# Four and a half chunks of twelve transposed by DMA instead of four

## The reference

```
layer 0:  s = x W0 inp^T, where adj > 0, else a very negative number
          x1 = layernorm(x + softmax(s / 0.07) inp)
layer 1:  Wh = x1 W;  e_ij = leaky_relu(Wh_i a1 + Wh_j a2), where adj > 0, else very negative
          out = layernorm(x1 + elu(softmax(e) Wh))
```

## Time and profile before

| | us |
|---|---|
| median of 3 executions | 1432.35 (1432.2 to 1432.74) |
| profiled execution | 1431.7 |
| its span, first to last instruction | 1429.9 |

### The profile page before, as it was taken

The page is one execution under the profiler, slowest core; times in us unless marked ns, Lnnn a source line. Parts: engine busy times, 40 slices in busy tenths (PEclk is TensorE's granted clock), DMA queues, the critical chain, the costliest instruction groups (busy, mean ns, idle before and its releaser), DMA issues.

```text
span 1429.9 us, 28561 instructions
## 1 busy us (share of the span) xinstructions
PE 1404.5 (98%) x9695; PEld 1012.5 (71%) x9695; DVE 1288.6 (90%) x2170; ACT 1103.4 (77%) x2477; POOL 1192.8 (83%) x895
## 2 busy tenths in 40 slices
PE   8999999999999999999999999999999999999997
PEld 4677777777777777777777777776666666676764
DVE  6999999999999999999899999979999999999997
ACT  6788888888888888888888888887856665666564
POOL 6878888888888888888888878857989999999995
PEclk9999999999999999999999999999999999999999
DMA  8999999999999999999899999857444444443520
GB/s 269 295 276 270 257 265 252 272 273 274 263 255 262 267 267 276 267 264 264 254 272 269 274 261 257 249 99 143 92 94 91 104 102 103 98 109 85 108 59 16
DMA packets 431761, 294.06 MB, mean 206 GB/s; under 512 B 360064, under 2 KB 406400, under 8 KB 431616
## 3 DMA queue, kind: packets, MB, share of 16 engines
q1 hardware_dynamic: 431616, 292.24, 75.5%
HBM read 163.19 MB, written 40.92 MB: 143 GB/s over the span
## 4 chain that ended last, share of the span: by engine, by line
PE 93%; DVE 3%; issue 1%; ACT 1%; POOL 1%; DMA 0%; POOLq 0%; DVEq 0%; SPq 0%; ACTq 0%
PE ps L698 17%; PE ps L783 12%; PE ps L727 12%; PE ps L793 11%; PE ps L700 9%; PE ps L738 8%; PE ps L740 8%; PE ps L739 8%; PE ps L764 6%; DVE rows L1130 1%; PE ps L665 1%; PE ps L807 1%; POOL p_lo L601 1%; DVE neg_mask L1095 1%; PE ps L658 0%
## 5 line engine op out<-in xcount | busy, mean ns | idle before, releaser
L935 ACT ACTIVATE rows<-rows,exp_bias 128x512 f32<-128x512 f32 x576 | 417.1, 724 | 55.9 <-DVE exp_bias L1105 55.8
L601 POOL TENSOR_TENSOR p_lo<-p,p_hi 128x1024 fp32r<-128x1024 f32 x171 | 403.0, 2406 | 26.6 <-ACT p_hi L983 22.9
L1130 DVE CUSTOM_DVE_ANT_0 rows<-ps,neg_mask 128x1024 f32<-128x1024 f32 x288 | 352.1, 1223 | 79.6 <-PE ps L740 72.1
L509 POOL TENSOR_SCALAR edges<-neg_mask 128x1536 uint8<-128x1536 bf16 x190 | 307.3, 1617 | 95.8 <-DVE neg_mask L1095 83.9
L1226 DVE SCALAR_TENSOR_TENSOR p<-ps,e_col,edgesT 128x1024 f32<-128x1024 f32 x288 | 348.8, 1274 | 5.6 <-ACT ps L988 4.6
L698 PE MATMUL ps<-vals,pT_hi 128*128 128x256 f16 x1536 | 294.6, 273 | 0.2
L921 ACT CAST pT_hi<-ps 128x512 f16<-128x512 f32 x384 | 222.9, 580 | 89.7 <-PE ps L727 89.5
L551 POOL TENSOR_TENSOR inp_sb<-rows,inp_sb 128x512 f16<-128x512 f32 x192 | 281.6, 1486 | 8.2 <-DVE inp_sb L1139 0.7
L700 PE MATMUL ps<-vals,pT_lo 128*128 128x128 f16 x1536 | 274.1, 219 | 0.0
L983 ACT CAST p_hi<-p 128x1024 fp32r<-128x1024 f32 x191 | 195.0, 1047 | 97.6 <-DVE p L1226 92.3
L1146 DVE TENSOR_TENSOR pT_lo<-ps,pT_hi 128x512 f16<-128x512 f32 x384 | 250.7, 683 | 3.7 <-ACT pT_hi L921 3.7
(11 more groups left out here) (130 smaller groups left out, 1934.7 us busy)
## 6 DMA issues: line engine op xcount, KB each, us to landing
adj_sb<-adj SPq DMA_DIRECT2D x192, 768.0 KB, 5.6
edge_rows<-edges SPq DMA_DIRECT2D x192, 192.0 KB, 4.8
xq<-x SPq DMA_DIRECT2D x48, 64.0 KB, 2.9
xr<-x SPq DMA_DIRECT2D x48, 64.0 KB, 5.7
r_wide<-r_rows SPq DMA_DIRECT2D x5, 512.0 KB, 4.0
out<-y_w SPq DMA_DIRECT2D x5, 512.0 KB, 3.7
inp_sb<-inp SPq DMA_DIRECT2D x3, 768.0 KB, 8.0
inp_sb<-inp_sb SPq DMA_TRANSPOSE x96, 4.6
```

What stands on the lines that cost most here:

```text
L601: nc.gpsimd.tensor_tensor(p1_lo[:, m % LO_SLOTS, :], p1[:, (NB * g + n) % P_SLOTS, :], p1_hi[:, m % HI_SLOTS, :].bitcast(F32), ALU.subtrac ...
L935: nc.scalar.activation(row_chunk(1 - par, c), row_chunk(1 - par, c), ACT.Exp, bias=exp_bias[:, 1 - par:2 - par], scale=EXP_SCALE, accum_ou ...
L1130: nc.vector.tensor_tensor_reduce(row_pair(par, k), scores_pair(k), neg_mask_row[:, 2 * k * CHUNK:2 * (k + 1) * CHUNK], 1.0, -3.0e38, ALU.a ...
```

## The change

The DMA way now takes four chunks and the first two of the four blocks of chunk 4 (EXTRA = 2): 2304 columns instead of 2048, in five pieces (PIECES), the fifth 256 wide. TensorE turns only the other two blocks of chunk 4, and the cast and the subtraction of this turn are 256 wide. ScalarE's fifth cast is at step 7; GpSimd's fifth low part stands between the fourth and the edges of the next tile. The product of the two blocks moves from chunk 4's attend (step 9) to that of chunk 3 (step 8). The waits that counted four pieces count five. `moved_lo` has a buffer of its own; `s_prod` lies in the end of the space of `inp_sb`.

```diff
+EXTRA = 2
-        MW = MOVED * CHUNK
+        PIECES = MOVED + 1
+        MW = MOVED * CHUNK + EXTRA * P
-        moved_hi, moved_lo = (inp_space[:, i * MW:(i + 1) * MW] for i in range(2))
-        movedT = inp_space[:, 2 * MW:6 * MW].rearrange(...)
+        moved_hi = inp_space[:, 0:MW]
+        moved_lo = sb0("moved_lo", [P, MW], F16)[:]
+        movedT = inp_space[:, MW:5 * MW].rearrange(...)
-        s_prod = sb0("s_prod", [P, 2, P], F32)
+        s_prod = inp_sb[:, NB - 2:NB, :]
+        def moved_piece(of, i):
+            return of[:, i * CHUNK:min((i + 1) * CHUNK, MW)]
+        def moved_rows(par, i):
+            return rows[:, par * N + i * CHUNK:par * N + min((i + 1) * CHUNK, MW)]
+        def turned_part(bc):
+            return slice(EXTRA * P if bc == MOVED else 0, CHUNK)
 # SP
-                    sp.wait_ge(moved_hi_set, MOVED * (tile + 1))
+                    sp.wait_ge(moved_hi_set, PIECES * (tile + 1))
-                    sp.wait_ge(moved_lo_set, MOVED * (tile + 1))
+                    sp.wait_ge(moved_lo_set, PIECES * (tile + 1))
 # GpSimd
-                if tile == 0:
-                    pool.wait_ge(vals_lo, MOVED)
-                nc.gpsimd.tensor_tensor(moved_lo[:, i * CHUNK:(i + 1) * CHUNK], row_chunk(tile % 2, i),
-                                        moved_hi[:, i * CHUNK:(i + 1) * CHUNK], ALU.subtract)
+                nc.gpsimd.tensor_tensor(moved_piece(moved_lo, i), moved_rows(tile % 2, i), moved_piece(moved_hi, i),
+                                        ALU.subtract)
                     moved_low(t - 1, 2)
                     moved_low(t - 1, 3)
+                    moved_low(t - 1, 4)
 # TensorE: attend, then the turn
-                for b in range(BPC):
-                    jb = bc * BPC + b
+                first = bc * BPC + (EXTRA if bc == MOVED else 0)
+                last = (bc + 1) * BPC + (EXTRA if bc == MOVED - 1 else 0)
+                for jb in range(first, last):
-                        for b in range(BPC):
+                        for b in range(EXTRA if bc == MOVED else 0, BPC):
 # ScalarE
-                        nc.scalar.copy(pT_hi[:, n % PT_SLOTS, :], ps[:, PT0 + n % NPT, :])
-                    if 0 <= c - LAG < MOVED and 1 <= t < NB:
+                        part = turned_part(bc)
+                        nc.scalar.copy(pT_hi[:, n % PT_SLOTS, part], ps[:, PT0 + n % NPT, part])
+                    if 0 <= c - LAG < PIECES and 1 <= t < NB:
 # VectorE
-                            if 2 * k < MOVED:
-                                dve.wait_ge(moved_lo_set, MOVED * (t - 1))
+                            if 2 * k <= MOVED:
+                                dve.wait_ge(moved_lo_set, PIECES * (t - 1))
-                        nc.vector.tensor_tensor(pT_lo[:, s, :], ps[:, PT0 + n % NPT, :], pT_hi[:, s, :],
+                        part = turned_part(bc)
+                        nc.vector.tensor_tensor(pT_lo[:, s, part], ps[:, PT0 + n % NPT, part], pT_hi[:, s, part],
```

More of the change, by code:

```diff
@@ L98, in build @@
         pT_lo = sb0("pT_lo", [P, PT_SLOTS, CHUNK], F16)
-        MW = MOVED * CHUNK
+        PIECES = MOVED + 1
+        MW = MOVED * CHUNK + EXTRA * P
         inp_space = inp_sb[:].bitcast(F16).rearrange("p b d -> p (b d)")
-        moved_hi, moved_lo = (inp_space[:, i * MW:(i + 1) * MW] for i in range(2))
-        movedT = inp_space[:, 2 * MW:6 * MW].rearrange("p (s h b m) -> p s h b m", s=2, h=2, m=P)
+        moved_hi = inp_space[:, 0:MW]
+        moved_lo = sb0("moved_lo", [P, MW], F16)[:]
+        movedT = inp_space[:, MW:5 * MW].rearrange("p (s h b m) -> p s h b m", s=2, h=2, m=P)
         xq = sb0("xq", [P, P], F32)
@@ L536, in score_cols @@
                 after(pool, s_set, j)
-                nc.gpsimd.tensor_tensor(s_prod[:], x1.rearrange("p (a d) -> p a d", a=1).to_broadcast([P, 2, P]), wa_rep[:],
+                nc.gpsimd.tensor_tensor(s_prod, x1.rearrange("p (a d) -> p a d", a=1).to_broadcast([P, 2, P]), wa_rep[:],
                                         ALU.mult).then_inc(s_prod_set, 1)
@@ L545, in moved_low @@
             def moved_low(tile, i):
-                pool.wait_ge(moved_hi_set, MOVED * tile + i + 1)
-                if tile == 0:
-                    pool.wait_ge(vals_lo, MOVED)
+                pool.wait_ge(moved_hi_set, PIECES * tile + i + 1)
                 if tile >= 1:
                     pool.wait_ge(movedT_in[(tile - 1) % 2], movedT_loads(tile - 1))
-                nc.gpsimd.tensor_tensor(moved_lo[:, i * CHUNK:(i + 1) * CHUNK], row_chunk(tile % 2, i),
-                                        moved_hi[:, i * CHUNK:(i + 1) * CHUNK], ALU.subtract).then_inc(moved_lo_set, 1)
+                nc.gpsimd.tensor_tensor(moved_piece(moved_lo, i), moved_rows(tile % 2, i), moved_piece(moved_hi, i),
+                                        ALU.subtract).then_inc(moved_lo_set, 1)
             def tile_rstd(t, par, known):
@@ L679, in attend @@
                 if t_of == 0:
-                    pe.wait_ge(vals_lo, bc + 1)
+                    pe.wait_ge(vals_lo, bc + 2 if bc == MOVED - 1 else bc + 1)
                     pe.wait_ge(wa_copied, 1)
@@ L692, in attend @@
                 acc = tile_sum(t_of)
-                for b in range(BPC):
-                    jb = bc * BPC + b
-                    cols = slice(b * P, (b + 1) * P)
+                first = bc * BPC + (EXTRA if bc == MOVED else 0)
+                last = (bc + 1) * BPC + (EXTRA if bc == MOVED - 1 else 0)
+                for jb in range(first, last):
+                    cols = slice((jb - bc * BPC) * P, (jb - bc * BPC + 1) * P)
                     p_hi = movedT[:, t_of % 2, 0, jb, :] if by_dma else pT_hi[:, s, cols]
                     p_lo = movedT[:, t_of % 2, 1, jb, :] if by_dma else pT_lo[:, s, cols]
-                    nc.tensor.matmul(acc, p_hi, vals[:, jb, :], start=(bc == MOVED and b == 0), stop=False,
+                    nc.tensor.matmul(acc, p_hi, vals[:, jb, :], start=(jb == MOVED * BPC + EXTRA), stop=False,
                                      skip_group_check=True)
                     mm = nc.tensor.matmul(acc[:, P:2 * P], p_lo, vals[:, jb, 0:P], start=False,
-                                          stop=(bc == MOVED - 1 and b == BPC - 1), skip_group_check=True)
+                                          stop=(jb == MOVED * BPC + EXTRA - 1), skip_group_check=True)
                 mm.then_inc(pv_done, 1)
@@ L920, in tile_steps @@
                             act.wait_ge(pv_done, attend_number((n - PT_SLOTS) // TURNS, (n - PT_SLOTS) % TURNS + MOVED) + 1)
-                        nc.scalar.copy(pT_hi[:, n % PT_SLOTS, :], ps[:, PT0 + n % NPT, :]).then_inc(pT_hi_set, 1)
-                    if 0 <= c - LAG < MOVED and 1 <= t < NB:
+                        part = turned_part(bc)
+                        nc.scalar.copy(pT_hi[:, n % PT_SLOTS, part], ps[:, PT0 + n % NPT, part]).then_inc(pT_hi_set, 1)
+                    if 0 <= c - LAG < PIECES and 1 <= t < NB:
                         i = c - LAG
@@ L928, in tile_steps @@
                             act.wait_ge(movedT_in[t % 2], movedT_loads(t - 2))
-                        nc.scalar.copy(moved_hi[:, i * CHUNK:(i + 1) * CHUNK], row_chunk(1 - par, i)).then_inc(moved_hi_set, 1)
+                        nc.scalar.copy(moved_piece(moved_hi, i), moved_rows(1 - par, i)).then_inc(moved_hi_set, 1)
                     if known is None or 1 <= known <= NB:
@@ L1134, in tile_steps @@
                         row_bias(t, par, known)
-                    if t == NB and 0 <= c - LAG < MOVED:
+                    if t == NB and 0 <= c - LAG < PIECES:
                         i = c - LAG
@@ L1138, in tile_steps @@
                         dve.wait_ge(movedT_in[t % 2], movedT_loads(t - 2))
-                        nc.vector.tensor_copy(moved_hi[:, i * CHUNK:(i + 1) * CHUNK], row_chunk(1 - par, i)).then_inc(moved_hi_set, 1)
+                        nc.vector.tensor_copy(moved_piece(moved_hi, i), moved_rows(1 - par, i)).then_inc(moved_hi_set, 1)
                     if turn_at(known, c):
```

## The result

The change makes the kernel slower: 1447.17 us (median of 4, 1446.42 to 1447.57) against 1432.28 us (median of 4), ratio 1.0104 (95% interval 1.0086 to 1.0121). The profiled execution took 1447.0 us, its span is 1445.2 us, 15.3 more than before. TensorE's granted clock is 0.996, as before.

The account below looks back on a forecast made before the run. A GpSimd-VectorE loop, 19.11 + 0.72 = 19.83 us per tile, was to overtake TensorE: 45 x 0.475 = 21.4, less 1.5 at the end, on 1431.7 gives 1451.6, 1452.3 as median. Range 1436 to 1462, likeliest case 1443 to 1461.

Parts of the forecast that it names:

- The ring becomes the bound: Per tile: the GpSimd-VectorE loop grows from 19.11 to 19.83 us, above TensorE's 19.14; +0.47 over 19.36; chance 0.70.
- The term of GpSimd's fifth part: GpSimd's new 256-wide low part, ahead of edges and sum: 0.65 us plus 0.07 of waiting, 0.72 per tile.
- the mask's wait: GpSimd's low parts beside VectorE's mask: the mask still delays the fourth, costing about 0.07 us more per tile.
- The end, -1.5 us: End of the first layer: TensorE's lead of up to 1 us and 0.22 in each of two last tiles save 1.5.
- the ring: Once-per-tile loop: GpSimd from mask to sum, VectorE from bn_stats to next mask; 19.11 us before the change.
- TensorE alone at 19.14: TensorE per tile: two of 32 transposes fewer save 0.22 us, so its own work falls from 19.36 to 19.14.
- rival A: Steps 8 to 11: the mask waits past the fourth low part, TensorE stays the bound, 1422 us; chance 0.13.
- ScalarE, VectorE, DMA at no cost: Casts under 0.1 us more, pT_lo 0.3 less, DMA work 19.1 per tile, later landing with 2.8 us left: hidden.
- rival C: Step 3: longer DMA transposes land 2.8 us later and ScalarE waits; above 1462 us; chance 0.05.

Follow-up runs that it names:

- before_extra_low: The kernel before, plus one 256-column GpSimd subtraction into an unread buffer, which the second DMA transpose and the masks' additions await: 1447.56 us, 1.0105.
- after_sum_first: The changed kernel with GpSimd's two additions of x and the product moved ahead of the next tile's two edges: 1435.46 us, 1.0024 to before.
- after_low_by_vector: The changed kernel with the fifth low part taken from GpSimd and given to VectorE at the end of step 9: 1434.38 us, 1.0015 to before.
- the dose: The kernel before with an extra GpSimd subtraction 32, 128 or 256 columns wide: 1431.89, 1435.87 and 1447.56 us.
- after_sum_lo_first: The changed kernel with GpSimd's two additions ahead of the edges and VectorE's step-9 pT_lo ahead of the mask's addition: 1420.68 us, 0.9919 to before.

## Why the prediction was right, and where it was off

*The ring becomes the bound.* Right, and shown three ways: before_extra_low makes the loss alone, after_sum_first and after_low_by_vector take most of it away, and the dose has a threshold near 0.26 with a slope of one beyond it. Its length of 19.11 without the new part stands: 19.68 - 0.56 = 19.12.

*The term of GpSimd's fifth part.* Mis-sized: 0.56 per tile, not 0.72. The operation took 0.667 where 0.69 was worked out, but the fourth part beside it became shorter, and the mask's wait, put at 0.07 more, did not grow. This is 0.16 x 45 = 7 us. That the mask, coming in the middle of the third low part, would go ahead of the fourth was right: the fourth and fifth took 2.51 us together from 344.26, 1.88 of them the fourth's.

```profile
343.73 1.38 DVE L1108 TENSOR_SCALAR neg_mask<-adj_sb 128x1536 bf16<-128x1536 int32 x1
```
```profile
344.26 2.51 POOL L561 TENSOR_TENSOR moved_lo<-rows,inp_sb 128x512 f16<-128x512 f32 x2
```

*The end, -1.5 us.* Wrong: it was +0.4 (15.3 less what 45 tiles brought: 0.86 at the first bn_stats and 44 x 0.32). The last three distances of bn_stats were 19.61, 12.43 and 8.13 before and are 19.31, 12.81 and 8.46 now. The first of them holds what TensorE had run ahead, 0.30 and not 1 us. The step let TensorE run until att_out holds it, but it stands earlier: at the turn of step 2, for which VectorE's pT_lo behind the waiting bn_stats must free the PSUM bank. In the changed kernel this pT_lo runs from 332.17 and the turn starts at 332.99.

```profile
332.17 0.68 DVE L1160 TENSOR_TENSOR pT_lo<-ps,pT_hi 128x512 f16<-128x512 f32 x1
```
```profile
332.99 0.63 PE L739 MATMUL ps<-ident,rows 128*128 128x128 f32 x4
```

The last two distances should have become 0.22 shorter each and became 0.38 and 0.33 longer, 0.7 together. It is no work of the ring: after_sum_lo_first, which is free of it, has 12.82 and 8.46 too, and before_extra_low has 12.44 and 8.13. In the last tile VectorE makes the casts for the DMA way, now five. They stand in the chain of work that ends the layer (the profile's view of that chain, start and us), where the kernel before has ScalarE's exponentials:

```profile
966.67 2.41 DVE inp_sb L1152 x2
```

The prediction did not look at these casts; that they are the cause was not tested. The two errors, 7 us too many for the fifth part and 2 too few at the end, have opposite signs and leave 1452 against 1447.

*TensorE alone at 19.14.* The sum of its work was right to 0.01, as after_sum_lo_first shows. That it would run at that rate with the ring out of the way was not: "four of them move from step 9 to step 8" was written down and not followed. The order of the work left a second bound at 19.39. That the forecast did not suffer from this is luck, since the ring at 19.68 covered it; rival A, 1422 by another order of the waits, would have met it too, as after_sum_first and after_low_by_vector did at 1435 and 1434.

*ScalarE, VectorE, DMA at no cost.* The new cast took 0.41 and the shortened one 0.36 where 0.3 each was put, still hidden. The second transpose landed 4.7 us after its issue, the share of the DMA engines is 0.95, and even at 1.00 in after_sum_lo_first no engine waited for a landing; rival C fails.

## What to carry to other kernels

An engine that is busy all of the time says where the time is now, not how far it may fall: look for every chain of waits that closes on itself once per tile, add up its links from the starts in the timelines, and compare the sum with the tile. Work that is added to an engine with idle time is not free when it stands ahead of the instruction that the ring waits for and is longer than the ring's slack. Two short additions moved ahead of 3 us of edges, which nobody waited for so early, took the loss from 1.0% to 0.2%, and one more pair in the other order made it a gain of 0.8%. And when a change moves work between the steps of one engine, follow the buffers with two slots on both sides of the move: each ties one step of an engine to another engine's work for a step two before, and a sum over the whole tile does not show it.

## What the hardware showed that was not expected

- The DMA engines' share reached 1.00 over 320 us at 277 GB/s without any engine waiting for a landing. By itself a share of 1.00 did not make them the bound.
- A mask on VectorE that is issued in the middle of a GpSimd subtraction goes ahead of the next subtraction, by the times: the mask came at 343.73 in the third low part and took 1.38, and the fourth, begun at 344.26, took 1.88 us where undisturbed ones take 1.15 to 1.16.
- GpSimd's subtraction with f16 out takes 243, 424 and 670 ns for 32, 128 and 256 columns: 1.9 ns per column over a base near 0.18 us.
